# Gathers of raw node rows: other row counts in the source view, and some tiles fetched in two gathers

## The chip, the cores and the metric

The kernel runs on one NeuronCore of a Trainium2 chip. The metric is the device time of one execution in microseconds (us). Engines: PE is TensorE (matmuls), DVE is VectorE, ACT is ScalarE, POOL is GpSimd, SP is SyncE, which here only issues DMAs. POOL issues all indirect DMAs (gathers of rows by index).

## The reference

One layer of a graph network over 12,500 nodes with 160 features and 412,500 edges sorted by destination:

```
h   = relu(layernorm(x))                                 # per node
l   = h @ W_l1 (64x64 for the scalars, 32x32 for each of three vector parts)
w   = relu(edge_attr_10 @ W_fc1 * c) * sqrt2 @ W_fc2 * c'   # 192 weights per edge
m   = products of w, l[edge_src] and edge_attr_4         # messages
s   = segment_sum(m, edge_dst) / 4
out = x + (h @ W_si) * node_vec + 0.5 * (s @ W_l2) * node_vec / sqrt(96)
```

## The kernel before

**Stage one: the table.** Node features `x` come in 14 chunks (`load_x`, L229). DVE computes the layer norm's statistics, ACT centres, PE transposes and multiplies by `W_l1` (L391 to L396), ACT scales the result into `ls` (three buffers, L346 to L353), and SP stores four tiles of 128 rows at a time into the DRAM tensor `l_table` (L507, 25 stores, q = 0 to 24). The table has NP = 12,544 rows: 98 tiles of 128, of which the last 44 rows are padding.

**Beside it: the raw rows.** For 21 of the 806 groups of edges (a group is four tiles of 128 edges, called a quad here) the gather isn't made from the table but from the raw input `xa` (rows of 160 features and the node's scalar, 161 elements), while the table is still being made. The loop at L255 to L263 issues them on POOL: quad r = 0 to 20, four gathers each of 128 rows (L260), into `ring`, which has NRB = 7 places in the tile ZD. From quad 7 on POOL waits until the quad seven places earlier has been stored from the ring to the DRAM tensor `raw_rows` (`raw_store`, L499, on SP's queue). SP waits for all gathers of a quad (semaphore `s_rg`) before it issues that store. The stores of quad r stand in SP's program between the table's stores: quad r follows the table store q at which 4r + 4 <= 3q, the rest follow the last table store. SP executes its program in order.

**Stage two: the groups.** POOL's program continues with the gathers from `l_table` (L819), after waits for the end of the table, its stores and a flag. 779 groups are fetched so, four tiles each (the last group has fewer), into six buffers in the tile R: POOL waits before a group for DVE's product of the group six earlier (semaphore `s_p`, L1028). 21 groups come from `raw_rows`, six from single-row DMAs that SP issues. For every group PE makes the 192 weights (L1095, L1105), ACT applies relu (L925), DVE multiplies weights and rows (L1025, L1028), PE sums by destination (L1118), ACT evacuates (L931) and SP stores (L850). Once per 128 nodes the sums are placed (L624, L639), multiplied by `W_l2` and stored. SP loads the edges' features for this stage (L830, L836) after its last raw store.

The order of work is written out by hand; nothing in it depends on measured or estimated costs.

Of the kernel before, what the change touches and what calls it, by code (L numbers as in the profile page):

```python
# [8 lines left out]
G = 4  # L9
# [36 lines left out]
def raws(n_nodes, n_edges):  # L46

    nt, ng = plan(n_nodes, n_edges)
    ready = due(n_nodes, n_edges)
    free = [ready[j] + 6 for j in range(nt - 1) if ready[j + 1] - ready[j] >= 8 and ready[j] + 13 < ng]  # L50
    n = min(NRAW, len(free) // 3)
    return [(free[i * len(free) // n], free[i * len(free) // n] + 6) for i in range(n)]


def single(n_nodes, n_edges):

    nt, ng = plan(n_nodes, n_edges)
    raw = [g for k, g in raws(n_nodes, n_edges)]
    n = min(NROW, len(raw))
    some = [raw[(i + 1) * len(raw) // n - 1] + 15 for i in range(n)] if n else []  # L60
    return [g for g in some if g < ng - 1]


def build(nc, a, n_nodes, n_edges):

    f32, i32, f32r = mybir.dt.float32, mybir.dt.int32, mybir.dt.float32r
# [4 lines left out]
    NP = NT * 128  # L71
# [13 lines left out]
    RAW = raws(n_nodes, n_edges)  # L85
    NR = len(RAW)
# [3 lines left out]
    NRB = 7  # L90
# [12 lines left out]
    with ctx:  # L103
        def sb(name, shape, dt=f32):
            return ctx.enter_context(nc.sbuf_tensor(name, shape, dt))
# [4 lines left out]
        def sem(name):  # L110
            return ctx.enter_context(nc.semaphore(name))

        x = sb("x", [128, NT, C])
        src_raw = sb("src_raw", [128, max(NR, 1) * G], i32)
        src_row = sb("src_row", [128, max(NRC, 1), RB], i32)
        src = sb("src", [128, NG * G], i32)
        rel = sb("rel", [128, NG, G])
# [44 lines left out]
        ring = ZD[:, 0:NRB * G * CR].rearrange("p (b t c) -> p b t c", b=NRB, t=G)  # L162
# [16 lines left out]
        V, PE, AC, SP, PL = nc.vector, nc.tensor, nc.scalar, nc.sync, nc.gpsimd  # L179
# [33 lines left out]
        s_rg = [sem(f"s_rg{b}") for b in range(NRB)]  # L213
# [23 lines left out]
        for r in range(NG * G * WIN, ROWS, 128):  # L237
            n = min(128, ROWS - r)
# [16 lines left out]
        for r in range(NR):  # L255
            if r >= NRB:
                PL.wait_ge(s_rs[r % NRB], 16 * (r // NRB))
            for t in range(G):
                k = r * G + t
                PL.indirect_dma_start(  # L260
                    out=ring[:, r % NRB, t, :], out_offset=None, in_=a["xa"],
                    in_offset=bass.IndirectOffsetOnAxis(ap=src_raw[:, k:k + 1], axis=0),
                ).then_inc(s_rg[r % NRB], 16)  # L263


        V.memset(zt[:, :, :], 0.0).then_inc(s_zero, 1)
# [41 lines left out]
        def blocks(q):  # L308

            return range(4 * q, min(4 * q + 4, NT))  # L310
# [184 lines left out]
        tv = T.rearrange("(j p) c -> p j c", p=128)  # L495

        def raw_store(r):
            SP.wait_ge(s_rg[r % NRB], 64 * (r // NRB + 1))
            SP.dma_start(W[r, :, :], ring[:, r % NRB, :, :].rearrange("p t c -> p (t c)")).then_inc(s_rs[r % NRB], 16)  # L499

        nrs = 0
        for q in range(NQ):
            n = len(blocks(q))
            if XC + q < NLC:
                load_x(XC + q)
            SP.wait_ge(s_lv, rows_out(q))
            SP.dma_start(tv[:, 4 * q:4 * q + n, :], ls[:, q % 3, 0:n, :]).then_inc(s_T[q % 3], 16)  # L507
            while nrs < NR and 4 * nrs + 4 <= 3 * q:
                raw_store(nrs)
                nrs += 1  # L510
        for r in range(nrs, NR):
            raw_store(r)
# [249 lines left out]
        with nc.If(way == 0):  # L762
# [48 lines left out]
            for g in range(NG):  # L811
                if g in raw_of or g in row_of:
                    continue
                for u in pairs(g):
                    if g >= NB:
                        PL.wait_ge(s_p, 2 * (g - NB) + u + 1)
                    for t in tiles(g, u):
                        k = g * G + t
                        PL.indirect_dma_start(  # L819
                            out=Y[:, g % NB, t, :], out_offset=None, in_=T,  # L820
                            in_offset=bass.IndirectOffsetOnAxis(ap=src[:, k:k + 1], axis=0),
# [179 lines left out]
            def slot(g, u):  # L1001

                return (2 * g + u) % 3
# [58 lines left out]
            for g in range(NG):  # L1062
                V.wait_ge(s_wp, g + 1)
                for u in pairs(g):
                    if u == pairs(g)[-1]:
                        i = slot(g, u)
# [125 lines left out]
        with nc.Else():  # L1192
# [33 lines left out]
            with nc.Fori(0, NG * G) as i:  # L1226
# [9 lines left out]
                for e in (PE, PL, V):  # L1236
                    e.wait_ge(f_ld, 80)
                PL.indirect_dma_start(out=Y[:, 0, 0, :], out_offset=None, in_=T,
                                      in_offset=bass.IndirectOffsetOnAxis(ap=one[:, 0:1], axis=0)).then_inc(f_g, 16)
# [6 lines left out]
                n = [0]  # L1246
# [17 lines left out]
                for k in range(4):  # L1264
                    PL.indirect_dma_start(out=cur[:, k, :], out_offset=None, in_=A4,
                                          in_offset=bass.IndirectOffsetOnAxis(ap=ix[:, 0, k:k + 1], axis=0)
# [25 lines left out]
                for k in range(4):  # L1292
                    PL.indirect_dma_start(out=A4, out_offset=bass.IndirectOffsetOnAxis(ap=ix[:, 1, k:k + 1], axis=0),
                                          in_=new[:, k, :], in_offset=None, bounds_check=NP * 4 - 1,
# [9 lines left out]
def lay_out(v, n_nodes, n_edges):  # L1304

    NT, NG = plan(n_nodes, n_edges)
    NP, EP = NT * 128, NG * GE
# [6 lines left out]
    src = np.zeros(EP, np.int32)  # L1314
# [10 lines left out]
    NR = -(-NG // 2)  # L1325
# [18 lines left out]
    k = 0.25 * 0.5 / np.sqrt(96.0)  # L1344
# [5 lines left out]
    for d in range(3):  # L1350
# [3 lines left out]
        r, t = 320 + 64 * d, 512 + 32 * d  # L1354
# [13 lines left out]
    bound = np.zeros((3, KB * 128), np.int32)  # L1368
    bound[:, :NG * G] = bases, low, high
    RAW = raws(n_nodes, n_edges)  # L1370
    src_raw = np.zeros((max(len(RAW), 1) * G, 128), np.int32)
    for r, (k, g) in enumerate(RAW):
        src_raw[r * G:(r + 1) * G] = src.reshape(-1, 128)[g * G:(g + 1) * G]
    ROW = single(n_nodes, n_edges)
    src_row = np.zeros((-(-max(len(ROW) * GE, 1) // (128 * RB)) * 128, RB), np.int32)
    for i, g in enumerate(ROW):
# [18 lines left out]
def program(nc, arrays, n_nodes, n_edges):  # L1395
    aps = {k: nc.dram_tensor("in_" + k, list(w.shape), mybir.dt.from_np(w.dtype), kind="ExternalInput").ap()
           for k, w in arrays.items()}
    aps["out"] = nc.dram_tensor("out", [plan(n_nodes, n_edges)[0] * 128, C], mybir.dt.float32,
                                kind="ExternalOutput").ap()
    build(nc, aps, n_nodes, n_edges)  # L1400
# [18 lines left out]
```

## Time and profile before

| what | value |
|---|---|
| median of 2 runs | 4031.9 us (4031.2 and 4032.61) |
| profiled execution, span from first to last instruction | 4036.8 us |
| POOL busy | 3034.7 us, 3203 instructions |
| PE busy | 3468.5 us |
| DVE busy | 2059.2 us |
| ACT busy | 1089.5 us |
| granted TensorE clock, mean | 0.805 of full speed |

The profiled execution's own time is known by its span, which is 4.9 us more than the median of the two runs. Busy times are of one engine; a gather on POOL is counted as busy only while POOL prepares it, and its data lands later. The rows of the section below are read from this execution.

### The profile page before, as it was taken

How to read it: one execution, taken by the hardware profiler on the slowest of the kernel's cores; microseconds unless marked ns; L12 is line 12 of the kernel's file. 1: busy time of each engine (PE TensorE's matmuls, PEld its weight loads, DVE VectorE, ACT ScalarE, POOL GpSimd, SP SyncE). 2: the span in 40 equal slices, each digit the busy share in tenths (PEclk: the TensorE clock that was granted, in tenths of full speed). 3: DMA queues.
4: the chain of work that ended last, by engine and by line, in shares of the span. 5: the costliest groups of instructions: out<-in, count | busy, mean ns of one | idle time of the engine just before them, and what ended most of it. 6: DMA issues, size and time to landing. Idle time of an engine off the chain costs nothing.

```text
span 4036.8 us, 67469 instructions
## 1 busy us (share of the span) xinstructions
PE 3468.5 (86%) x17464; PEld 2022.3 (50%) x17464; DVE 2059.2 (51%) x7424; ACT 1089.5 (27%) x2487; POOL 3034.7 (75%) x3203
## 2 busy tenths in 40 slices
PE   5788888888888888888888888888888898888888
PEld 4455445445444545555555545554455454555444
DVE  7454545455445545555455454555455554545554
ACT  5222222222222222222222222222222222222222
POOL 6777777777777777777777777777777777777776
PEclk8788878788778878787887787878788887878887
DMA  9455555555555555555555555555555555555554
GB/s 315 141 148 139 137 142 136 144 143 136 136 139 142 138 142 137 140 138 145 136 144 136 141 134 143 139 140 141 138 143 137 144 137 144 136 142 134 143 145 124
DMA packets 725181, 581.64 MB, mean 144 GB/s; under 512 B 393834, under 2 KB 648126, under 8 KB 724414
## 3 DMA queue, kind: packets, MB, share of 16 engines
q1 hardware_dynamic: 568800, 308.24, 28.3%
q0 software_dynamic: 153552, 262.31, 26.6%
q10 hardware_dynamic: 2446, 6.71, 0.4%
q8 instruction: 151, 2.47, 0.3%
q14 instruction: 232, 1.90, 0.2%
HBM read 421.86 MB, written 155.04 MB: 143 GB/s over the span
## 4 chain that ended last, share of the span: by engine, by line
POOL 38%; DMA 25%; issue 15%; DVE 11%; PE 11%; ACT 0%; DVEq 0%; SPq 0%; POOLq 0%; ACTq 0%
POOL R L819 37%; DMA R<-l_table,src 24%; DVE R L1028 6%; DVE R L1025 4%; PE bank L1105 3%; PE bank L639 3%; PE bank L1118 2%; PE bank L1095 2%; POOL ZD L260 1%; DMA raw_rows<-ZD 0%; PE bank L662 0%; DMA x<-in_xp 0%; DVE R L1014 0%; PE bank L682 0%; DVE st L279 0%
## 5 line engine op out<-in xcount | busy, mean ns | idle before, releaser
L819 POOL DMA_INDIRECT R<-l_table,src x3115 | 2952.8, 948 | 950.2 <-issue 772.4
L1025 DVE TENSOR_TENSOR R<-bank,R 128x256 f32<-128x256 f32 x1600 | 676.9, 423 | 1889.1 <-DMA R<-l_table,src 1288.1
L1105 PE MATMUL bank<-w,hs 100*128 100x192 f32 x6446 | 1536.0, 388 | 88.4 <-DVE R L1028 86.7
L1105 PEld LDWEIGHTS bank<-w,hs 100*128 100x128 f32 x6446 | 1285.6, 228 | 493.4 <-issue 483.4
L1118 PE MATMUL bank<-R 128*32 128x320 f32 x6448 | 740.6, 536 | 419.2 <-DVE R L1028 417.4
L1028 DVE TENSOR_TENSOR R<-bank,R 128x192 f32<-128x192 f32 x3200 | 978.0, 347 | 0.0
L931 ACT ACTIVATE E<-bank 128x320 f32<-128x320 f32 x806 | 352.7, 438 | 2177.3 <-PE bank L1118 2133.0
L1095 PE MATMUL bank<-ea,w1s 10*100 10x512 f32 x1612 | 561.4, 779 | 10.3 <-DMA ea<-in_ea_p 9.5
L925 ACT ACTIVATE hs<-bank 100x512 f32<-100x512 f32 x806 | 437.5, 594 | 393.1 <-PE bank L1095 393.1
L1118 PEld LDWEIGHTS bank<-R 128*32 128x32 f32 x6448 | 149.7, 117 | 659.8 <-issue 658.6
L639 PE MATMUL bank<-ZD 128*128 128x448 f32 x776 | 393.8, 660 | 0.0
L639 PEld LDWEIGHTS bank<-ZD 128*128 128x128 f32 x776 | 172.7, 235 | 246.6 <-issue 246.6
L1095 PEld LDWEIGHTS bank<-ea,w1s 10*100 10x100 f32 x1612 | 121.0, 189 | 278.0 <-issue 267.7
L1014 DVE TENSOR_TENSOR R<-bank,e 128x128 f32<-128x128 f32 x806 | 234.8, 291 | 27.4
L682 PEld LDWEIGHTS bank<-pw,zt 128*128 128x128 f32 (+1 forms) x970 | 158.6, 218 | 69.7 <-issue 69.7
L682 PE MATMUL bank<-pw,zt 128*128 128x160 f32 (+1 forms) x970 | 184.7, 345 | 0.0
L1011 DVE TENSOR_TENSOR bank<-bank,rel 128x32 f32<-128x32 f32 x806 | 152.9, 190 | 0.0
L644 ACT ACTIVATE zz<-bank 128x448 f32<-128x448 f32 x98 | 53.3, 544 | 307.5 <-PE bank L639 305.3
L260 POOL DMA_INDIRECT ZD<-in_xa,src_raw x84 | 81.8, 973 | 34.2 <-issue 25.0
L624 DVE SCALAR_TENSOR_TENSOR ZD<-pos,bank 128x256 f32<-128x256 f32 x196 | 72.7, 412 | 0.0
L662 PEld LDWEIGHTS bank<-ident,zz 128*128 128x128 f32 x392 | 41.1, 140 | 63.0 <-issue 62.6
L662 PE MATMUL bank<-ident,zz 128*128 128x128 f32 x392 | 64.2, 286 | 0.2 <-ACT zz L644 0.2
(109 smaller groups left out, 829.3 us busy)
## 6 DMA issues: line engine op xcount, KB each, us to landing
s_tiles<-E SPq DMA_DIRECT2D x806, 160.0 KB
R<-l_table,src POOLq DMA_INDIRECT x3115
ea<-in_ea_p SPq DMA_DIRECT2D x403, 96.0 KB
ZD<-s_tiles SPq DMA_DIRECT2D x392, 96.0 KB, 2.5
ZD<-s_tiles SPq DMA_DIRECT2D x97, 320.0 KB
psc<-l_table SPq DMA_DIRECT2D x1536, 0.6 KB
H<-l_table SPq DMA_DIRECT2D x1536, 0.6 KB
ZD<-s_tiles SPq DMA_DIRECT2D x391, 48.0 KB, 3.1
```

Source lines behind the costliest of these rows:

```text
L639: m = PE.matmul(bank[7][:, 0:448], D[:, j % 2, c, :], Z[:, j % 2, c, :], start=c == 0, stop=c == NCH - 1)
L682: m = PE.matmul(home(j, placed)[:, 0:C], turned(j, placed, q)[0:n, :], pw[0:n, q, :], start=q == 0, stop=q == 4)
L819: PL.indirect_dma_start(out=Y[:, g % NB, t, :], out_offset=None, in_=T, in_offset=bass.IndirectOffsetOnAxis(ap=src[:, k:k + 1], axis=0),). ...
L925: AC.activation(hs[:, g % 4, :], bank[g % 2][0:100, 0:GE], ACT.Relu, scale=REL).then_inc(s_hs, 1)
L931: AC.activation(E[:, g % 3, :], bank[5 + g % 2][:, 0:2 * C], ACT.Copy).then_inc(s_e, 1)
L1011: V.tensor_tensor(oh[i], steps[i][:, 0:WIN].unsqueeze(1).to_broadcast([128, G, WIN]), rel[:, g, :].unsqueeze(2).to_broadcast([128, G, WIN] ...
L1014: V.tensor_tensor(S[:, g % 2, :, :].rearrange("p t (n k) -> p t n k", k=4), oh[i].unsqueeze(3).to_broadcast([128, G, WIN, 4]), e4[:, c % 2 ...
L1025: V.tensor_tensor(p[:, :, :, 0:64], w[:, :, 0:128].rearrange("p t (s c) -> p t s c", s=2), y[:, :, 0:64].unsqueeze(2).to_broadcast([128, n ...
L1028: m = V.tensor_tensor(p[:, :, s, 64:160].rearrange("p t (d c) -> p t d c", d=3), w[:, :, 128 + 32 * s:160 + 32 * s].unsqueeze(2).to_broadc ...
L1095: m = PE.matmul(bank[i][0:100, 0:GE], w1s[r, :], ea[r, p % 3, :], start=True, stop=True)
L1105: m = PE.matmul(b[:, o * 192:(o + 1) * 192], hs[:, g % 4, t * 128:(t + 1) * 128], w2[:, :], start=True, stop=True, skip_group_check=True)
L1118: m = PE.matmul(b[q, 0:2 * C], S[:, g % 2, t, :], P[:, g % 2, t, :], start=True, stop=True)
```

## The change

The 21 quads of raw rows are treated by r mod 7. Remainders 0 to 4 (15 quads, r = 0 to 4, 7 to 11, 14 to 18) still have four gathers of 128 rows each, but `in_` is a view of the first 12,544 - 0, 8, 4, 2 or 1 rows. No index is above 12,499, so the same rows are read. Remainder 5 (r = 5, 12, 19) makes two gathers per tile, for partitions 0 to 63 and 64 to 127; remainder 6 (r = 6, 13, 20) makes two per tile for partitions 0 to 95 and 96 to 127; the indices of each gather stand in a column of their own that begins at partition 0. `src_raw` has 108 columns where it had 84. The semaphore targets count the added gathers.

```diff
+def cuts(r):
+
+    return {5: ((0, 64), (64, 128)), 6: ((0, 96), (96, 128))}.get(r % 7, ((0, 128),))
+
+
+def cut_columns(n):
+
+    out = []
+    for r in range(n):
+        for t in range(G):
+            for i, (p, e) in enumerate(cuts(r)):
+                out.append((r, t, i, p, e))
+    return out
+
+
+def view_rows(r, rows):
+
+    return rows - (0, 8, 4, 2, 1)[r % 7] if r % 7 < 5 else rows
...
-        src_raw = sb("src_raw", [128, max(NR, 1) * G], i32)
+        CUT = cut_columns(NR)
+        ncut = [0] * NRB
+        arrived = []
+        for r in range(NR):
+            ncut[r % NRB] += 16 * G * len(cuts(r))
+            arrived.append(ncut[r % NRB])
+        src_raw = sb("src_raw", [128, max(len(CUT), 1)], i32)
...
-            for t in range(G):
-                k = r * G + t
-                PL.indirect_dma_start(
-                    out=ring[:, r % NRB, t, :], out_offset=None, in_=a["xa"],
-                    in_offset=bass.IndirectOffsetOnAxis(ap=src_raw[:, k:k + 1], axis=0),
-                ).then_inc(s_rg[r % NRB], 16)
+            for k, (rr, t, i, p, e) in enumerate(CUT):
+                if rr != r:
+                    continue
+                if e - p < 128:
+                    PL.indirect_dma_start(
+                        out=ring[p:e, r % NRB, t, :], out_offset=None, in_=a["xa"],
+                        in_offset=bass.IndirectOffsetOnAxis(ap=src_raw[0:e - p, k:k + 1], axis=0),
+                    ).then_inc(s_rg[r % NRB], 16)
+                else:
+                    PL.indirect_dma_start(
+                        out=ring[:, r % NRB, t, :], out_offset=None, in_=a["xa"][0:view_rows(r, NP), :],
+                        in_offset=bass.IndirectOffsetOnAxis(ap=src_raw[:, k:k + 1], axis=0),
+                    ).then_inc(s_rg[r % NRB], 16)
...
-            SP.wait_ge(s_rg[r % NRB], 64 * (r // NRB + 1))
+            SP.wait_ge(s_rg[r % NRB], arrived[r])
```

## Rows read from the trace of the kernel before

**Rows 1.** The page, parts 1 and 4: busy time by engine; the chain that ended last.

```profile
PE 3468.5 (86%) x17464; PEld 2022.3 (50%) x17464; DVE 2059.2 (51%) x7424; ACT 1089.5 (27%) x2487; POOL 3034.7 (75%) x3203
...
POOL 38%; DMA 25%; issue 15%; DVE 11%; PE 11%; ACT 0%; DVEq 0%; SPq 0%; POOLq 0%; ACTq 0%
```

**Rows 2.** Groups by line on POOL: count, busy us, mean ns, idle before, releasers.

```profile
L819 POOL DMA_INDIRECT R<-l_table,src x3115 | 2952.8, 948 | 950.2 <-issue 772.4 <-DVE R L1028 177.8
L260 POOL DMA_INDIRECT ZD<-in_xa,src_raw x84 | 81.8, 973 | 34.2 <-issue 25.0 <-DMA raw_rows<-ZD 6.6 <-DMA src_raw<-in_src_raw 2.6
```

**Rows 3.** The instructions of L819, and the waits on POOL (total, times, longest us).

```profile
L819 POOL DMA_INDIRECT R<-l_table,src x3115: 942/949/964, 116.8 to 4018.5; - x195
...
POOL R L819 <- DVE R L1028: 177.8, 583, 0.3
```

**Rows 4.** The instructions of L260: duration ns min/median/max, starts; time to landing.

```profile
L260 POOL DMA_INDIRECT ZD<-in_xa,src_raw x84: 942/949/1483, 3.1 to 115.5; - x84
...
DMA to landing us min/median/max: 2.6/5.5/8.8
```

**Rows 5.** POOL in order of time: start us, busy us, and idle before it.

```profile
51.12 0.94 POOL L260 DMA_INDIRECT ZD<-in_xa,src_raw  x1 [0.30 <-issue]
52.36 0.95 POOL L260 DMA_INDIRECT ZD<-in_xa,src_raw  x1 [0.31 <-issue]
59.92 0.94 POOL L260 DMA_INDIRECT ZD<-in_xa,src_raw  x1 [6.61 <-DMA raw_rows<-ZD]
...
115.51 0.95 POOL L260 DMA_INDIRECT ZD<-in_xa,src_raw  x1 [0.30 <-issue]
116.77 0.95 POOL L819 DMA_INDIRECT R<-l_table,src  x1 [0.30 <-issue]
...
146.83 0.94 POOL L819 DMA_INDIRECT R<-l_table,src  x1 [0.31 <-issue]
```

**Rows 6.** SP's queue in order of time: start us, us, what it issues.

```profile
40.94 12.52 SPq L499 DMA_DIRECT2D raw_rows<-ZD  x1
...
54.03 1.54 SPq L499 DMA_DIRECT2D raw_rows<-ZD  x1
...
99.98 0.84 SPq L499 DMA_DIRECT2D raw_rows<-ZD  x1
...
106.41 0.60 SPq L499 DMA_DIRECT2D raw_rows<-ZD  x1
107.17 0.79 SPq L507 DMA_DIRECT2D l_table<-ls  x1
108.00 10.46 SPq L499 DMA_DIRECT2D raw_rows<-ZD  x4
119.52 0.33 SPq L836 DMA_DIRECT2D e<-in_e_t  x1
```

**Rows 7.** The chain that ended last, in order of time: start us, us, what.

```profile
40.94 18.72 DMA raw_rows<-ZD
```

**Rows 8.** The page, part 3: the gathers' DMA queue: packets, MB, share of 16 engines.

```profile
q0 software_dynamic: 153552, 262.31, 26.6%
```

**Rows 9.** POOL by stretches: length, busy us (count), clock, DMA share, GB/s.

```profile
3.00:53.50 50.50, 38.33 (x40) 0.92 1.09 367
...
60.00:116.50 56.50, 43.35 (x44) 0.91 0.88 276
116.70:4019.50 3902.80, 2952.77 (x3115) 0.80 0.55 140
```

**Rows 10.** DVE and PE at the start of stage two, in order of time.

```profile
131.78 0.61 DVE L1028 TENSOR_TENSOR R<-bank,R 128x192 f32<-128x192 f32 x2
...
133.07 0.61 DVE L1028 TENSOR_TENSOR R<-bank,R 128x192 f32<-128x192 f32 x2
...
123.25 2.03 PE L1095 MATMUL bank<-ea,w1s 10*100 10x512 f32 x4 [9.46 <-DMA ea<-in_ea_p]
```

**Rows 11.** The table's stores, L507: time from issue to landing.

```profile
DMA to landing us min/median/max: 2.5/4.5/21.0
```

More of the change, by code:

```diff
@@ L1370, in lay_out @@
     RAW = raws(n_nodes, n_edges)
-    src_raw = np.zeros((max(len(RAW), 1) * G, 128), np.int32)
-    for r, (k, g) in enumerate(RAW):
-        src_raw[r * G:(r + 1) * G] = src.reshape(-1, 128)[g * G:(g + 1) * G]
+    CUT = cut_columns(len(RAW))
+    src_raw = np.zeros((max(len(CUT), 1), 128), np.int32)
+    for c, (r, t, i, p, e) in enumerate(CUT):
+        src_raw[c, 0:e - p] = src.reshape(-1, 128)[RAW[r][1] * G + t, p:e]
     ROW = single(n_nodes, n_edges)
```

## The prediction

> **What bounds the kernel now.** The busy shares come first, and they mislead: PE is busy 86% and POOL 75%, but the chain that ended last has POOL, DMA and "issue" in 78% of it and PE in 11% [rows 1]. So read POOL's groups. Its two kinds of gather leave 0.30 us of idle before each, put down to "issue"; where a product of DVE is named as releaser the wait is never longer than 0.3 us, which is that same gap, so POOL waits for nobody in stage two [rows 2, 3]. From 116.77 to 4018.5 us it issues 3115 gathers: 3901.7 / 3114 = 1.253 us each, 0.949 busy and 0.304 gap [rows 3, 5]. Everything else follows it, and 18.3 us of tail come after the last gather's start (4036.8 - 4018.5). What the reader is to see: POOL is one unbroken row of gathers, and a microsecond put before the first L819 is a microsecond at the end.
>
> In stage one the row has one hole. After 40 gathers (quads 0 to 9) POOL waits 6.61 us, 0.30 of it gap, so 6.3 us are lost, until 59.92 us: quad 10 wants quad 3's place in the ring, whose store was issued at 40.94 us and landed 18.72 us later [rows 5 to 7]. The last raw gather starts at 115.51 and the first table gather directly at 116.77 with only the gap before it [rows 5], so the table is not what POOL waits for: its last store is issued at 107.17 [rows 6].
>
> **The change, part by part.**
>
> *24 gathers more.* Six quads go from four gathers to eight. What a gather of 32, 64 or 96 rows costs POOL the trace doesn't show; all have 128. Lower bound: the busy 0.949 is all work per row, and a tile in two gathers pays only one more gap, 0.304 us; 24 x 0.304 = 7.3 us. Upper bound of the rows: none of it depends on the row count; 24 x 1.253 = 30.1 us. I choose near the upper end, five sixths of the busy time fixed: 0.304 + 0.79 = 1.10 us, 26.4 us in all. What leans me there is that the busy time stands at 942 to 949 ns for rows of 644 bytes and of 640, at a DMA share of 1.09 and of 0.55 [rows 3, 4, 9]: it looks like a set-up, not like work that follows the data. This is a judgement and not a measurement. A small gather dearer than a whole one has no row for it and is not excluded; the top of the range carries it.
>
> *The hole closes.* Quads 5 and 6 now bring 8 more gathers ahead of quad 10. POOL would have been ready at 59.92 - 6.31 = 53.6 us; with 8 x 1.10 it is ready at 62.4, after the landing at 59.7, if that stands. So 6.3 us are given back. At the lower bound it is ready at 56.0, and only 2.4 are.
>
> *Views with fewer rows, 60 gathers, of which 12 have none left out.* The rows read, their number and their bytes are the same, POOL issues as many instructions, and nothing on DVE, PE, ACT or SP is added. I cost the views at nothing on POOL. The trace has one shape of view for L260 and nearly the same for L819, so it cannot show what the row count of a view does.
>
> Here a rule speaks against the change. The trace shows a gather of 128 rows taking 0.266 x 16 x 4036.8 / 3199 = 5.37 us of engine time in sum, and landing 2.6 to 8.8 us after its issue [rows 4, 8]; spread over all 16 engines the 5.37 are 0.34 us. The Trainium skill ("DMA: Bandwidth & Descriptors", "Why a DMA increments its semaphore by 16 and not by 1") says that a DMA is spread over the largest number of engines up to 16 that divides the outermost size of both access patterns. By that rule 12,544 rows give 16, and views 8, 4, 2 and 1 rows shorter give 8, 4, 2 and 1 engines, while pieces of 64, 96 and 32 rows keep 16. No row here shows whether a gather counts the view or the indices. By the rule the sum moves only if POOL or the stores feel it (first rival below).
>
> *Stores and SP's queue.* A raw store waits for its quad's last gather. Shifts of POOL, with 4.4 us for each split quad and less the 6.3: 2.5 us in quads 7 to 11, 6.9 at 12, 11.3 at 13 to 18, 15.7 at 19, 20.1 at 20. Before, quads 14 to 16 had their last gathers at about 85, 90 and 95 us; now at 96, 101 and 106, landing 5.5 later at 101.5, 106.5 and 112, against stores that SP reached at 100.0, 104.5 and 106.4 [rows 4, 6]. Queued behind the wait of quad 16 is the last table store: 107.17 moves to about 112.5 and lands, at the median 4.5, at 117 [rows 11]. POOL then needs the table only at 116.8 + 20.1 = 136.9: covered, with 20 us to spare. If that cover is gone (a store held 20 us), POOL would wait at the first L819.
>
> *Start of stage two.* SP's edge loads come behind the last raw store, at 119.52, 2.8 us after POOL's first table gather; they move with POOL. PE starts at 123.25, DVE's first group is done by 133.7, and POOL first needs that at its 25th gather, at 146.83, so 13 us are to spare in which a colder PE can be slow [rows 5, 6, 10]. Cost nothing. The larger index load (108 columns for 84) is before the first gather at 3.1 us; a few tens of ns at most.
>
> **The sum.** 26.4 - 6.3 = +20.1 us, on the span 4036.8 to 4056.9, and on the median, which is 4.9 lower, 4031.9 to 4052.0 us. Ends by the row prices: 7.3 - 2.4 = +4.9 (4037) and 30.1 - 6.3 = +23.8 (4056).
>
> **The rivals.**
>
> *Fewer engines per gather, POOL untouched (chance 0.20).* The data of one gather then sits 5.37 us on one engine, 2.7 on two. POOL runs 4 to 5 gathers ahead of the landing already (5.5 us against 1.253), so it need not notice. The DMA share is 1.09 until 53.5 us [rows 9], so the loads of x on the loaded engines slip by up to 5.4 us, and with them quad 3's store: it lands at 65.0, POOL arrives at 62.4 and waits 2.6 again. Time 4052 to 4055. For it: the row counts are powers of two short of a multiple of 16, and the page. Against: no row.
>
> *A small gather is priced by its rows (0.17).* 4037 to 4044: the low half of the bounds. For it: the busy time may be 128 rows of work, at 7.4 ns each; the trace can't refute that.
>
> *Slower: POOL is held by gathers on few engines (0.09).* Place: L260 in quads 1 to 4, 8 to 11 and 15 to 18, 48 gathers. If POOL could not go on before the engines had room, a gather on one engine would take 5.37 us for 1.253, on two 2.69, on four 1.34: 12 x (4.12 + 1.43 + 0.09) = +68 us, 4120. It decides from (80.6 - 20.1) / 48 = 1.26 us more for each of the 48: from there the kernel is over 2% slower. For it: L260's mean busy time is 973 ns against the 948 of L819, its longest 1483 [rows 2, 4], so POOL is held a little now and then while the DMA engines are crowded. Against it: there a landing takes four periods and POOL still keeps its period. Over 2% in about half of this case.
>
> *Not slower: views make a gather cheaper on POOL (0.07).* If part of the 0.949 us is spent per engine, gathers on 1 to 8 engines save it. It decides from 20.1 / 48 = 0.42 us for each, nearly half of the busy time; time 4032 or less. Nothing in the trace speaks for it.
>
> **How the numbers follow.** The forecast, views free and small gathers near the whole price, has 0.47 and 4046 to 4057 as its own range. The range of 8 in 10 goes from 4037, the lower bound of the pieces' price, to 4067, which holds the first rival, a small gather dearer than a whole one by up to 0.45 us (24 x 0.45 = 10.8 above 4056), and the mild third of the slower case; left out are the not-slower case and the rest of the slower one. Two per cent, 80.6 us, is what a measurement of this kernel can tell from no change: slower by it 0.05, from the held POOL alone; faster by it 0.01, since stage one's POOL has only 113 us to lose; within it 0.94.
>
> **What would show it.** The first L819 starts at about 136.9 us instead of 116.77, and 3115 gathers still take 3901.7 us. L260 has 108 instructions; the small ones' busy time gives the price, 0.79 us for my fixed part alone and about 0.87 on a mean for 64 rows, 0.475 if priced by rows, 0.949 if not at all. The wait before the first gather of quad 10 is gone (first rival: it stays, under 3 us). For the engines: the gather queue's packets stand at 48 per gather (153,552 / 3199) [rows 8]; if views set the engines, L260's landing grows well beyond 8.8 us in quads 4, 11 and 18, and the busy time of the 12 gathers of each view differs or not, which tells the third rival from the fourth. My prediction is wrong if the first L819 isn't shifted by what the added gathers cost, or if stage two's period changes.

## The result, and the profile after

The changed kernel takes 4054.96 us (median of 2 runs, 4053.16 and 4056.76) against 4031.9: +23.1 us, a ratio of 1.0058 with a 95% interval of 1.004 to 1.0075. Forecast was +20.1 us. It is slower by more than the runs scatter and by less than 2%.

The profiled execution after has a span of 4049.1 us and an own time of 4053.16 us, so 4.1 us lie around the span. The page of the kernel after, parts 1 and 3 (part 3: packets, MB, share of 16 engines):

```profile
span 4049.1 us, 67493 instructions
PE 3464.3 (86%) x17464; PEld 2024.0 (50%) x17464; DVE 2055.9 (51%) x7424; ACT 1088.7 (27%) x2487; POOL 3047.0 (75%) x3227
...
q0 software_dynamic: 153936, 262.31, 27.1%
```

Only POOL's count has changed, by 24 instructions (3203 to 3227). The groups of POOL in the kernel after (count | busy us, mean ns | idle before, releasers); L852 is the table gather (L819 before), L293 the whole raw gather, L288 the raw gather of fewer than 128 rows:

```profile
L852 POOL DMA_INDIRECT R<-l_table,src x3115 | 2944.8, 945 | 949.3 <-issue 793.9 <-DVE R L1061 155.4
L293 POOL DMA_INDIRECT ZD<-in_xa,src_raw x60 | 57.7, 961 | 20.7 <-issue 18.0 <-DMA src_raw<-in_src_raw 2.7
L288 POOL DMA_INDIRECT ZD<-in_xa,src_raw x48 | 44.3, 923 | 14.6 <-issue 14.6
```

The releaser "DMA raw_rows<-ZD" of [rows 2], the wait before quad 10, is gone. Shown in order of time on POOL, kernel after: first row the last whole gather of quad 4, then the first of quad 5 (64 rows), of quad 6 (96 and 32 rows), and the 48 gathers that stand before quad 10 run through without a hole; the last two rows are the end of stage one:

```profile
27.13 0.95 POOL L293 DMA_INDIRECT ZD<-in_xa,src_raw  x1 [0.30 <-issue]
28.38 0.90 POOL L288 DMA_INDIRECT ZD<-in_xa,src_raw  x1 [0.30 <-issue]
...
38.03 0.92 POOL L288 DMA_INDIRECT ZD<-in_xa,src_raw  x1 [0.30 <-issue]
39.25 0.86 POOL L288 DMA_INDIRECT ZD<-in_xa,src_raw  x1 [0.30 <-issue]
...
61.56 0.95 POOL L293 DMA_INDIRECT ZD<-in_xa,src_raw  x1 [0.30 <-issue]
62.81 0.95 POOL L293 DMA_INDIRECT ZD<-in_xa,src_raw  x1 [0.30 <-issue]
...
136.91 0.87 POOL L288 DMA_INDIRECT ZD<-in_xa,src_raw  x1 [0.30 <-issue]
138.08 0.95 POOL L852 DMA_INDIRECT R<-l_table,src  x1 [0.30 <-issue]
```

The first table gather has moved from 116.77 [rows 5] to 138.08: 21.3 us. Nothing else makes up this shift in this pair of traces: the busy time of raw gathers went from 81.8 to 57.7 + 44.3 us, +20.2; the idle time before them, the first one's left out, from 25.0 + 6.6 to 18.0 + 14.6, +1.0 (24 gaps more, one hole less); the start is 0.1 later. Stage two did not get longer. The instructions of L852, kernel after, and POOL's waits for DVE there (total, times, longest us), still never longer than the gap:

```profile
L852 POOL DMA_INDIRECT R<-l_table,src x3115: 942/946/962, 138.1 to 4031.0; - x195
...
POOL R L852 <- DVE R L1061: 155.4, 510, 0.3
```

4031.0 - 138.1 = 3892.9 us for 3115 gathers, 1.250 us each, where the profiled execution before had 3901.7 and 1.253 [rows 3]. So the spans differ by 12.3 us only: the profiled execution before was itself some 9 us slow in stage two. With the 4.1 us around the span it took about 4041 us, not the 4032 of its timed runs. A comparison of the two spans would halve the effect; the start of stage two, or the timed runs, give it rightly.

SP's queue after, answering to [rows 6] (start us, us, what it issues; L532 the raw stores, L540 the table's):

```profile
40.90 10.98 SPq L532 DMA_DIRECT2D raw_rows<-ZD  x1
...
100.15 0.34 SPq L532 DMA_DIRECT2D raw_rows<-ZD  x1
100.98 2.46 SPq L540 DMA_DIRECT2D l_table<-ls  x2
107.47 0.34 SPq L532 DMA_DIRECT2D raw_rows<-ZD  x1
...
111.32 0.34 SPq L532 DMA_DIRECT2D raw_rows<-ZD  x1
111.70 0.44 SPq L540 DMA_DIRECT2D l_table<-ls  x1
115.55 23.97 SPq L532 DMA_DIRECT2D raw_rows<-ZD  x4
140.57 0.33 SPq L869 DMA_DIRECT2D e<-in_e_t  x1
```

Quad 3's store went out at the same 40.9 us as before. The time from its issue to its landing, of this one store:

```profile
DMA to landing us min/median/max: 17.7/17.7/17.7
```

So its place was free at 58.6 us, and POOL came to it at 62.8, with 4 us to spare (forecast: 59.7 and 62.4). The last table store moved from 107.17 to 111.70, for a forecast 112.5, and landed 3.7 us later, 22 us before POOL needs it.

### The profile page after: what moved, and what is told of

Same layout as the page of the kernel before. It is cut to its first block, busy times and chain, and to the rows that moved or that the text cites. A ratio compares the mean times of both kernels' runs of the same rounds, so it can differ in the third digit from the quotient of the medians.

```text
span 4049.1 us, 67493 instructions
## 1 busy us (share of the span) xinstructions
PE 3464.3 (86%) x17464; PEld 2024.0 (50%) x17464; DVE 2055.9 (51%) x7424; ACT 1088.7 (27%) x2487; POOL 3047.0 (75%) x3227
## 4 chain that ended last, share of the span: by engine, by line
POOL 41%; DMA 22%; issue 15%; PE 12%; DVE 10%; DVEq 0%; ACT 0%; SPq 0%; POOLq 0%
POOL R L852 38%; DMA R<-l_table,src 22%; DVE R L1061 5%; PE bank L1138 4%; DVE R L1058 4%; PE bank L672 3%; PE bank L1151 2%; PE bank L1128 2%; POOL ZD L293 1%; POOL ZD L288 1%; PE bank L715 0%; PE bank L695 0%; DVE R L1047 0%; DVE bank L1044 0%; DVEq L1110 0%
## 5 line engine op out<-in xcount | busy, mean ns | idle before, releaser
L852 POOL DMA_INDIRECT R<-l_table,src x3115 | 2944.8, 945 | 949.3 <-issue 793.9
L1151 PE MATMUL bank<-R 128*32 128x320 f32 x6448 | 729.2, 529 | 423.9 <-DVE R L1061 422.1
L1128 PE MATMUL bank<-ea,w1s 10*100 10x512 f32 x1612 | 552.9, 767 | 29.5 <-DMA ea<-in_ea_p 28.7
L672 PE MATMUL bank<-ZD 128*128 128x448 f32 x776 | 414.5, 689 | 0.0
L672 PEld LDWEIGHTS bank<-ZD 128*128 128x128 f32 x776 | 181.2, 247 | 262.1 <-issue 262.1
L293 POOL DMA_INDIRECT ZD<-in_xa,src_raw x60 | 57.7, 961 | 20.7 <-issue 18.0
```

Source lines behind the costliest of these rows:

```text
L672: m = PE.matmul(bank[7][:, 0:448], D[:, j % 2, c, :], Z[:, j % 2, c, :], start=c == 0, stop=c == NCH - 1)
L852: PL.indirect_dma_start(out=Y[:, g % NB, t, :], out_offset=None, in_=T, in_offset=bass.IndirectOffsetOnAxis(ap=src[:, k:k + 1], axis=0),). ...
L1128: m = PE.matmul(bank[i][0:100, 0:GE], w1s[r, :], ea[r, p % 3, :], start=True, stop=True)
L1151: m = PE.matmul(b[q, 0:2 * C], S[:, g % 2, t, :], P[:, g % 2, t, :], start=True, stop=True)
```

## The experiments

Seven kernels ran, two of them more than once: ten runs in three groups, each group on a chip of its own. On all three chips the kernel before takes 5174 to 5182 us (medians of 15 to 22 executions), 28% more than above, at a mean granted clock of 0.73 to 0.75 for 0.805 above. The change was measured there too and takes 29% more. This is called the slower setting below; no experiment ran in the first one. What differs is seen in the third run, whose stage one is that of the kernel before. POOL's waits there (total us, times, longest):

```profile
POOL R L819 <- DVE R L1028: 1184.4, 413, 10.0
POOL R L819 <- issue: 843.4, 2701, 1.5
POOL ZD L260 <- DMA raw_rows<-ZD: 43.5, 5, 13.9
...
POOL R L819 <- DMA l_table<-ls: 7.9, 1, 7.9
```

A gather still takes POOL 948 ns and 0.30 of gap, but now POOL waits: 1184 us for DVE in stage two, where before no wait was over 0.3 us [rows 3], and five times for the ring in stage one. The other engines pause without anything to wait for that the profile shows, as PE does here for 12.7 us (third run, PE in order of time):

```profile
108.28 0.90 PE L396 MATMUL bank<-bl,htb 128*128 128x160 f32 x2 [12.71 <-issue]
```

Why these runs have such pauses is not in the traces. Ratios are within one group, and the prices of gathers carry over; the waits don't. A table of what follows below. The shift is that of the first table gather against the third run's; each time is read from one trace, and traces of the same kernel differ by up to 3.6 us (188.5 to 192.1), so a shift is good to some 3 us.

| run | first table gather, us | shift | ratio, 95% interval |
|---|---|---|---|
| third, `e3` (stage one as before) | 159.6 | | 0.9999 (0.9976 to 1.0021) |
| `e1` views alone | 161.0 | +1.4 | 0.9999 (0.9984 to 1.0015) |
| `e7` the change | 189.6 | +30.0 | 1.0061 (1.0047 to 1.0076) |
| `e2`, `e2b`, `e10` late cuts | 188.5, 190.5, 192.1 | +28.9 to +32.5 | 1.0061, 1.009, 1.0067 |
| `e6` four pieces | 253.7 | +94.1 | 1.019 (1.0175 to 1.0204) |
| `e4` odd pieces | 256.3 | +96.7 | 1.0209 (1.0176 to 1.0241) |
| `e5`, `e9` early stores | 157.6, 160.3 | -2.0, +0.7 | 0.9986, 1.0009 |

In all of these the table gathers then take 4964 to 4988 us, from the first start to the last, with no trend in the shift. So here too, where POOL isn't the only thing that sets stage two, a later start of its gathers goes through to the end.

**1. The views alone.**

```diff
 def cuts(r):
-    return {5: ((0, 64), (64, 128)), 6: ((0, 96), (96, 128))}.get(r % 7, ((0, 128),))
+    return ((0, 128),)
```

> All 21 quads in four gathers of 128 rows, but with the shortened views (8, 4, 2, 1 rows left out) of the change. Theory A (views cost nothing, the whole +23 us is the added small gathers): 4032 us, ratio 1.000 within 0.001; 84 gathers at 0.95 us; the wait of some 6 us before quad 10 is back; first table gather at 116 to 117 us; 153,552 packets in the gathers' queue, landing not over 9 us. Theory B (part of the change's cost is the views'): 4035 to 4045 us, with a busy time above 0.95 us in the shortened quads. Theory C (the view's row count sets how many DMA engines a gather uses): another packet count, landings well over 9 us in quads 4, 11 and 18, time 4032 to 4035.

Measured: 5173.8 us against 5174.08. The group of its raw gathers:

```profile
L293 POOL DMA_INDIRECT ZD<-in_xa,src_raw x84 | 80.4, 957 | 71.0 <-DMA raw_rows<-ZD 44.5 <-issue 23.8 <-DMA src_raw<-in_src_raw 2.6
...
q0 software_dynamic: 153552, 262.31, 20.7%
```

957 ns on a mean against 965 of the third run's, packets as before to the last one. That settles the price on POOL and theory B. For theory C look at the DMA engines while quad 18's four gathers, through the view of 12,543 rows, are the only traffic (131.4 to 137.8 us, 40 slices, mean busy share of the 16 engines in tenths; then packets, MB and share):

```profile
DMA  0008631000095210000942100038610000000000
...
q0 software_dynamic: 193, 0.33, 21.2%
```

Each gather shows as a spike of four slices of 0.16 us, up to eight or nine tenths. One engine alone could bring the mean of 16 to 0.6 of a tenth and would need 5.4 us for each. So a gather through a view with an odd number of rows still runs on nearly all engines: theory A holds for the views, B and C fall. The expected absolute times and the single wait of 6 us don't apply to the slower setting.

**2. The view in stage two**, to have its effect 3115 times instead of 60.

```diff
-    out=Y[:, g % NB, t, :], out_offset=None, in_=T,
+    out=Y[:, g % NB, t, :], out_offset=None, in_=T[0:NP - 1, :],
```

> The kernel before, with all 3115 table gathers reading through a view of the first 12,543 rows of the table (one padding row left out). Theory A (a view's row count does nothing): 4032 us, ratio 1.000 within 0.001, 153,552 packets, 0.95 us busy each. Theory C (the view's row count sets the number of DMA engines: one for an odd count): 5.37 us of engine time of each gather on one engine; packets change, DVE's waits for landing grow from 1288 us, time +5 us if POOL isn't held and several thousand us more if it is.

Measured: 5176.45 against 5174.08, ratio 0.9999. The page's line of its table gathers, and the queue:

```profile
L819 POOL DMA_INDIRECT R<-l_table,src x3115 | 2952.3, 948 | 2035.8 <-DVE R L1028 1184.4 <-issue 843.4 <-DMA l_table<-ls 7.9
...
q0 software_dynamic: 153552, 262.31, 20.6%
```

An odd number of rows in the view, 12,543, changes neither POOL's 948 ns nor one packet. The engine time of a gather is 0.206 x 16 x 5174.0 / 3199 = 5.33 us, before 5.37. With the busy DMA engines of experiment 1: the view's row count is not what a gather is divided by.

**3. Odd pieces**: full views, the number of rows gathered varied instead.

```diff
 def cuts(r):
+    q = (128, 125, 126, 124, 120, 100, 112)[r % 7]
+    return ((0, q), (q, 128)) if q < 128 else ((0, 128),)
```

> Full views; quads by r mod 7 in pieces of 128; 125 + 3; 126 + 2; 124 + 4; 120 + 8; 100 + 28; 112 + 16 rows: 72 tiles in two gathers. Theory A (busy time 0.84 us fixed and about 0.11 for 128 rows, whatever the count): 72 x 1.15 = 83 us more less the 6.3 of the ring wait, 4109 us. Theory C (here the number of rows gathered sets the engines: one for 125, two for 126, four for 124 and 100, eight for 120): packets per pair differ, landings of the 125-row gathers near 5.25 us above the others (11 us and more while x is loaded), and 4109 us if POOL isn't held; up to 4160 if it is, with busy times over 1 us in quads 1, 8 and 15.

Measured: 5280.2 us, +106. POOL in order of time, the first pair of gathers of quads 1 to 6 (of quad 5 a later pair), so 125 + 3, 126 + 2, 124 + 4, 120 + 8, 100 + 28 and 112 + 16 rows:

```profile
8.38 1.21 POOL L289 DMA_INDIRECT ZD<-in_xa,src_raw  x1 [0.30 <-issue]
9.90 0.90 POOL L289 DMA_INDIRECT ZD<-in_xa,src_raw  x1 [0.30 <-issue]
...
19.17 0.98 POOL L289 DMA_INDIRECT ZD<-in_xa,src_raw  x1 [0.31 <-issue]
20.45 0.89 POOL L289 DMA_INDIRECT ZD<-in_xa,src_raw  x1 [0.31 <-issue]
...
29.07 1.29 POOL L289 DMA_INDIRECT ZD<-in_xa,src_raw  x1 [0.30 <-issue]
30.66 0.89 POOL L289 DMA_INDIRECT ZD<-in_xa,src_raw  x1 [0.30 <-issue]
...
40.22 0.99 POOL L289 DMA_INDIRECT ZD<-in_xa,src_raw  x1 [0.30 <-issue]
41.51 0.90 POOL L289 DMA_INDIRECT ZD<-in_xa,src_raw  x1 [0.30 <-issue]
...
50.23 1.00 POOL L289 DMA_INDIRECT ZD<-in_xa,src_raw  x1 [0.30 <-issue]
51.53 0.90 POOL L289 DMA_INDIRECT ZD<-in_xa,src_raw  x1 [0.30 <-issue]
...
60.22 0.93 POOL L289 DMA_INDIRECT ZD<-in_xa,src_raw  x1 [0.30 <-issue]
61.45 0.86 POOL L289 DMA_INDIRECT ZD<-in_xa,src_raw  x1 [0.30 <-issue]
```

112 and 16 rows stand on the line of 128, 96, 64 and 32. Counts that aren't multiples of 16 lie above it: 120 and 100 rows take more than 128 do (0.949), 125 rows 1.21 and 124 rows 1.29. The order isn't that of the engines by the rule (1, 2, 4, 8 for 125, 126, 124, 120), so a price per engine saved or a POOL held by a full engine does not fit either: 125 would have to be the dearest. The added POOL work, with these durations, is 12 x (1.45 + 1.22 + 1.53 + 1.25 + 1.25 + 1.13) = 94 us, and its waits are 53.8 us for the third run's 51.4; together 96 of the 96.7 us of shift. Theory A's 83 us of added POOL work are too low by this term, the odd counts.

Whether the odd counts use fewer DMA engines is only made likely. Between 196.3 and 206.8 us nothing but quads' 124 + 4 runs on the DMA queues, between 228.2 and 236.9 nothing but 112 + 16. The mean busy share of the 16 engines in tenths, and GB/s in 40 slices, first for 124 + 4, then for 112 + 16, and the packets of each stretch:

```profile
DMA  0000000060022100004401220000070022200003
GB/s 0 3 3 0 0 0 0 2 56 0 17 86 111 49 0 0 0 0 55 37 17 69 93 49 0 0 0 0 1 57 17 17 86 76 66 0 0 0 0 36
...
q0 software_dynamic: 437, 0.26, 12.3%
...
DMA  0020000571000400005800002000058000020000
GB/s 0 0 65 18 0 0 0 124 187 21 0 0 0 48 0 0 0 0 145 187 0 0 0 3 45 0 0 0 0 145 166 21 0 0 0 45 3 0 0 0
...
q0 software_dynamic: 224, 0.27, 14.1%
```

In each pair of 124 + 4 most bytes (49 to 111 GB/s) come in three slices of 0.26 us at only one or two tenths, which is some three engines of 16, beside a spike of four to seven tenths that carries less (37 to 57 GB/s). The 112 rows come as one spike of two or three slices of 0.22 us, up to eight tenths and 187 GB/s, with half the packets. That is how a gather on a part of the engines would look, but which engines worked is not in these views. The views of experiments 1 and 2 changed no packet.

**4. Four pieces of 32 rows** in the quads with r mod 7 = 5 or 6, full views.

```diff
-    return {5: ((0, 64), (64, 128)), 6: ((0, 96), (96, 128))}.get(r % 7, ((0, 128),))
+    return tuple((p, p + 32) for p in range(0, 128, 32)) if r % 7 > 4 else ((0, 128),)
```

> Full views; the tiles of the six quads with r mod 7 = 5 or 6 in four gathers of 32 rows: 72 added gathers. Theory A (0.865 us busy and 0.304 gap for 32 rows, nearly all of it fixed): 24 x (4 x 1.169 - 1.250) = +82.2 us, less 6.3 for the ring wait: +76 us, first table gather near 193 us. Theory B (price by rows): 24 x 3 x 0.304 = 21.9 less up to 6.3: +16 to 22 us.

Measured: 5277.82 us against 5181.89, +96 us. The instructions of its pieces:

```profile
L288 POOL DMA_INDIRECT ZD<-in_xa,src_raw x96: 860/865/1156, 28.6 to 239.3; - x96
```

A quarter of the rows takes 91% of the time. The 72 added gathers bring 24 x (4 x 1.169 - 1.250) = 82.2 us of POOL work, and its waits before table gathers and for the ring are 63.6 us (42.0 + 8.1 + 13.5) for 51.4: 94.4 of the 94.1 us of shift. Theory B, 16 to 22 us, is out by a factor of four. The 6.3 us given back are not seen here; the waits grew instead.

**5. The cuts behind the hole.** If the added gathers of quads 5 and 6 were partly free because POOL would have waited anyway, the same number behind the wait must cost more.

```diff
 def cuts(r):
-    return {5: ((0, 64), (64, 128)), 6: ((0, 96), (96, 128))}.get(r % 7, ((0, 128),))
+    return ((0, 64), (64, 128)) if 14 <= r < 20 else ((0, 128),)
```

> Full views; six quads in gathers of 64 + 64 rows as in the change, but quads 14 to 19, behind the wait for the ring instead of quads 5, 6, 12, 13, 19, 20. 24 more gathers at 2 x (0.902 + 0.304) - 1.250 = 1.16 us a pair: +27.9 us. Theory A (in the change 6.3 us were given back because added gathers stood ahead of the ring wait): the wait is back, the first table gather starts near 144.5 us, time 4060 us. Theory B (the wait doesn't matter for the time of unprofiled runs, or the table stage grows by itself): +21 to 23 us as in the change, 4053 to 4055.

> The kernel of the late cuts once more (quads 14 to 19 in 64 + 64 rows, full views), beside the change itself on the same chip. Theory A (added gathers ahead of the ring wait are partly free, behind it they are not): +27.9 us, about 6 us more than the change. Theory B (the wait doesn't matter): as the change, within 2 us.

> The late cuts once more, for the same reason. On a chip of the first kind, theory A: the wait before quad 10 is back, first table gather at 144 to 145 us, time 4059 to 4061 us; theory B (the wait doesn't matter): 138 us and 4053 to 4055 us. On the slower kind again the first table gather near 190 us and 30 to 45 us more than before.

And beside the second of them the change itself:

> The change itself, beside the others on one chip. Expected from its trace: the first table gather moves by 21.3 us, so +21 to +23 us on a chip where POOL's gathers set stage two; where something else sets it, POOL's delay at the start of stage two still moves everything that follows, and the difference is the same within the noise.

Measured: late cuts 5209.94 against 5174.08, 5227.4 against 5181.89 and 5213.23 against 5178.97 us, ratios 1.0061 (1.0036 to 1.0086), 1.009 (1.0075 to 1.0106) and 1.0067 (1.0044 to 1.0089); the change 5214.31 against 5181.89, 1.0061 (1.0047 to 1.0076). In the one group that had both, the late cuts are 13 us above the change; over the three the intervals overlap it, and the first table gathers are within 3 us of the change's. POOL's waits of the change in the slower setting:

```profile
POOL ZD L293 <- DMA raw_rows<-ZD: 38.3, 4, 15.2
...
POOL R L852 <- DMA l_table<-ls: 9.9, 1, 9.9
POOL ZD L288 <- DMA raw_rows<-ZD: 6.6, 1, 6.6
```

54.8 us, for 51.4 in the third run: nothing is given back. So the change moves the first table gather by 30.0 us here and by 21.3 in its first trace. The difference of 8.7 us holds the 6.3 that the prediction counted as given back, and more: where the stores themselves come late, POOL waits for the ring however many gathers stand before. But late and early cuts can't be told apart in this setting, and the test of the 6.3 us by cuts stays inconclusive. What shows them is the kernel after's trace in the first setting alone: the wait of 6.61 us is not there, with the store issued at an unchanged 40.9 us and landed 4 us before POOL came.

**6. The stores earlier**, as another way to close the hole, and the version that might have beaten both kernels.

```diff
-            while nrs < NR and 4 * nrs + 4 <= 3 * q:
+            while nrs < NR and 4 * nrs + 1 <= 3 * q:
```

> The kernel before, with SP's raw stores placed earlier in its program (4r + 1 <= 3q for 4r + 4 <= 3q), no gather changed. Theory A (the ring wait before quad 10 costs 6.3 us of the time and can be closed without added gathers): quad 3's store goes out some 7 us earlier, the wait shrinks to at most 2 us, and the first table gather starts when the table has landed, at 111 to 113 us for 116.8: 4 to 6 us less, ratio 0.9985 to 0.999. Theory B (SP is held by the full DMA queue in any order, so the store lands at the same time): no difference, ratio 1.000.

> The early raw stores once more, in the hope of a chip of the first kind (before at about 4032 us). Theory A (the ring wait can be closed): quad 3's store goes out near 34 us instead of 40.9, no or little wait before quad 10, first table gather at 111 to 113 us for 116.8, time 4026 to 4028 us. Theory B (the full DMA queue holds SP in any order): 4032 us. On the slower kind (before at about 5175 us) again 2 to 10 us less, not clear of the noise.

Measured: 5171.9 against 5181.89 us (0.9986, 0.9972 to 1.0) and 5181.82 against 5178.97 (1.0009, 0.9988 to 1.003). Quad 3's store went out at 66.31 and 60.02 us, in the third run (another chip) at 70.06. In the second of the two the wait before quad 10 was down to 1.45 us, but 7.9 us then came before quad 11: the hole moved on. The ring waits fell in sum only from 43.5 to 39.1 and 40.0 us, but the wait for the table before the first table gather rose from 7.9 to 11.4 and 11.7: what POOL gained it lost to the table, which comes last here. No gain is shown. In the first setting, where the table landed at 111.7 us and POOL was ready at 116.5, it remains untried.

## Why the prediction was right

**The bound.** Right. POOL's row of gathers sets the end; the first table gather moved by 21.3 us and the runs by 23.1, with an interval (16 to 30 us from the ratio's) that holds both. In the slower setting 30.0 us of shift came out as 32.4.

**The price of a small gather, 1.10 us for each added one.** Right in kind and 5% low. A pair of 64 rows is 2 x (0.902 + 0.304) - 1.250 = 1.16 us more than a whole gather, 96 + 32 rows 0.913 + 0.865 + 0.608 - 1.250 = 1.14. 24 of them are 27.6 us for a forecast 26.4. The fixed part of the busy time is 0.84 to 0.85 us (16 rows: 0.86), nine tenths where five sixths were chosen. The choice was called a judgement, and no row had a piece; the reason given, that the busy time doesn't follow the data, held for multiples of 16 rows and would have failed for other counts (experiment 3). Three pieces ran longer, up to 1.71 us, and so did two whole gathers, up to 1.67, besides the first; in the kernel before six did, up to 1.48. Over the medians such gathers add about 2 us to either trace, so by luck they are not in the difference.

**The hole, 6.3 us given back.** Right in the first setting, read from one trace: the store landed at 58.6 us for 59.7, POOL came at 62.8 for 62.4. Arithmetic: 27.6 - 6.3 = 21.3. It is not a property of the change: in the slower setting, where the stores come late, it isn't given back. A run that puts the same gathers behind the hole in the first setting is missing.

**The views at nothing.** Right, shown by experiments 1 and 2. The first rival, fewer engines per gather by the view's rows, is out: experiment 1 left all packets as they were and shows gathers through 12,543 rows on nearly all engines. In the kernel after, no whole gather that the trace resolves took over 6.4 us to land, where the prediction named well over 8.8 as the sign; for quads 4, 11 and 18 this trace has no landings. The Trainium skill ("DMA: Bandwidth & Descriptors", "Why a DMA increments its semaphore by 16 and not by 1") has the number of engines divide the outermost size of both access patterns; for the source of a gather the measurement disagrees. For the number of rows gathered, the other pattern, experiment 3 shows that counts other than multiples of 16 cost more, in busy time and in packets. The busy times do not follow the number of engines that the rule gives (one for 125 rows at 1.20 us, four for 124 at 1.28, four for 100 at 0.99).

**Price by rows** (second rival) is out by experiment 4. **POOL held by few engines** and **cheaper views** are out with experiment 1: no busy time moved.

**SP and the start of stage two.** The table store came at 111.7 us for 112.5, covered as said; PE and DVE had no part.

**A weak spot** was the sum's base. The forecast took the profiled span as 4.9 us over the median, without the time around the span. It was an execution about 9 us slower than the timed runs, in stage two. The difference of two sums didn't suffer from it.

## What to carry to other kernels

An indirect gather costs GpSimd nearly the same for 16 rows as for 128, some 1.15 to 1.25 us with its gap; where its queue sets the time, count gathers, not rows, and keep the rows of each a multiple of 16, which was cheaper in every count tried here from 100 rows up. Added work is free only as far as it fills a wait whose release doesn't depend on it: look which store ends the wait, and what that store waits for. And compare the time at which the bounding queue starts its long stage before comparing spans, since one profiled execution can be 9 us off its own kernel's runs.

## What the runs showed of the hardware

GpSimd's busy time for a gather of f32 rows of 644 bytes: 0.85 to 0.86 us for 16 rows, 0.865 for 32, 0.902 for 64, 0.91 for 96, 0.93 for 112, 0.949 for 128; but 0.98 for 126, 0.99 for 120 and 100, 1.20 for 125 and 1.28 for 124. A source view of 12,543 rows leaves a gather on nearly all DMA engines (up to nine tenths of the 16 busy). Pieces of 2 to 8 rows take 0.88 to 0.90, more than 16 rows do. The kernel before took 4032 us in one setting and 5174 to 5182 in another, with POOL's gathers at the same 0.948 us in both and pauses of 10 us and more on PE, ACT and DVE; their cause stays open.
